# A new prologue for a convolution-and-three-mixes kernel: coefficient tables by full float32 matmuls over nine rows

## The chip, the cores and the metric

The kernel runs on one core of a Trainium2 chip. The metric is the device time of one execution in microseconds (us). Before the change it is 364.62 us, the median of three executions (364.05 to 366.46).

## What is computed

`x` is 128 samples of 64 channels by 1024 positions, all in float32. Four residual layers follow each other. The first is a grouped convolution with nine taps plus a bias that depends on the sample; each of the other three multiplies a sample by a 64 x 64 matrix of its own, which is a softmax-weighted mean of eight given matrices, and adds a bias of its own.

```python
# layer 0
x = x + (conv1d(x, weight, groups=4, pad=4) + (c @ c_weight.T)[:, :, None] + bias[None, :, None])
# layers 1, 2, 3, each with weights of its own
h = gelu(c @ W0 + b0); h = gelu(h @ W1 + b1)
att = softmax(h @ W2 + b2)                      # 128 samples x 8
agg_w = einsum('bk,koi->boi', att, weight)      # 128 matrices of 64 x 64
x = x + (einsum('boi,bih->boh', agg_w, x) + (att @ bias_k)[:, :, None])
```

## The kernel before

The three mixing layers are linear, so each sample needs only the product of its three matrices (each with the identity added) and one bias column. The work has two parts.

**The prologue** makes, for all 128 samples at once, what depends on the condition `c` alone. TensorE runs the three small networks (lines 405 to 421), VectorE and ScalarE the softmax. Then come the *tables* (line 98): `table[n]` holds the 64 x 64 matrix of layer n for every sample. They are made in 24 *banks* (`NTAB`, 8 for each layer), numbered t. A bank is four matmuls (L455) of a piece of `mixtab`, stationary, with the transposed attention `att_t`, moving, into one bank of PSUM (the 2 MiB memory that TensorE writes). Four copies of 64 x 256 then carry it into `table[n]`, on ScalarE (ACT, L576) and VectorE (DVE, L758). `ACT_ALONE` and `DVE_ALONE` name the banks that one of the two copies alone; of every other bank each copies a half. Five banks of PSUM go round, so bank t waits for the copies of bank t-5.

The matmuls of the tables are in the one-pass type fp32r. For accuracy, matrices and attention are each split into a high and a low part, and three products are added by laying the parts in three groups of 9 rows (8 matrices and the identity): partitions 0 to 26 of `mixtab`, with the other partitions set to zero. The rows get there in two steps: `mats` (432 KB) is loaded from memory over 108 partitions, DVE splits it (L710, L712), and three transfers within the chip's SBUF lay it out again, over 9 partitions each (L238). Later the same memory, `mixtab`, holds the `y` tiles of the main loop; so y moves wait for the first eight banks (L243).

**The main loop** goes over 32 steps q of four samples. A step loads `x` (L208), splits it (x_high L514 on ACT, x_low L649 on DVE or L324 on POOL), convolves it in four groups g of six matmuls (`conv`, L360) with the tap matrices `toep_hi` and `toep_lo`, copies the result (L521), moves it within SBUF (L222), composes the sample's matrices (L368, L378), and multiplies (`mix`, L400 to L402). The tap matrices are made in the prologue too: DVE adds an identity (L717), ACT makes the high part (L560) and DVE the low part (L725).

Each engine works its own list in order, and the lists are woven by hand. While the tables are made, `CONV_AFTER` puts a convolution group (q, g) behind a bank, `BIAS_PRODUCTS` and `BIAS_TURNS` put pieces of the bias chain (L430, L434, and `bias_sum`, L693 to L706, on DVE) there, and `SPLIT_AT` the splits of x. `POOL_LOW` names the steps whose low part POOL makes. Once all 24 banks are copied, POOL makes the last inputs of `compose_upper` (L311) and the main loop's first `mix` starts. All transfers go through the one queue of SyncE (SP), in program order.

Of the kernel before, what the change touches and what calls it, by code (L numbers as in the profile page):

```python
# [37 lines left out]
JX = J + 1  # L38
S = 4
# [3 lines left out]
K = 8  # L43
KR = K + 1
PARTS = 3
NL = 3
N = S * J
NH = C // 2
NG = 4
TG = NH // NG  # L50
NTAB = NL * TG
BIAS_TURNS = (4, 12)
BIAS_PRODUCTS = (8, 15)

CONV_AFTER = {1: (0, 0), 2: (0, 1), 3: (0, 2), 4: (0, 3), 9: (1, 0), 11: (1, 1), 13: (1, 2), 14: (1, 3), 19: (2, 0), 22: (2, 1)}
SPLIT_AT = {0: 1, 9: 2, 18: 3}
POOL_LOW = (1,)
ACT_ALONE = (8, 10, 12, 20)
DVE_ALONE = (2, 3, 5, 9, 11)
YHIGH_AT = 19  # L60
CH = 12
CW = NL * NH * 2 * C // CH

# [7 lines left out]
def columns(tile, widths):  # L71

    out, at = {}, 0
    for name, n in widths.items():
        out[name] = tile[:, at:at + n]
        at += n
    return out


def cond_resid_kernel(nc, x_h, net_h, kept_h, row_h, toep_h, mixrow_h, mats_h, out_h):  # L80
    with ExitStack() as ctx:
        def sb(name, shape, dt=F32):
# [31 lines left out]
        mixtab = sb("mixtab", [128, NL, NH, 2 * C], F32R)  # L114
# [6 lines left out]
        att_pad = sb("att_pad", [B, NL, 128], F32R)  # L121
        att_parts = att_pad[:, :, 0:PARTS * KR].rearrange("b n (t k) -> b n t k", t=PARTS)
        att_t = sb("att_t", [128, NL, B], F32R)
# [16 lines left out]
        mats = x_sb[:, 1].rearrange("p g s j -> p (g s j)")[0:KR * CH, 0:CW]  # L140
        mats_hi = conv_sb[:, 1].rearrange("p g n -> p (g n)")[0:KR * CH, 0:CW].bitcast(F32R)
        mats_lo = out_sb[:, 0].rearrange("p s n -> p (s n)")[0:KR * CH, 0:CW].bitcast(F32R)
        vadd = out_sb[:, 0].rearrange("p s n -> p (s n)")[:, CW:CW + C]

        second = columns(out_sb[:, 1].rearrange("p s n -> p (s n)"), dict(TOEP, hid1=NL * B, hid2=NL * B))
        toep, eye_tap = second["toep"], second["eye_tap"]
        toep_all = out_sb[:, 1].rearrange("p s n -> p (s n)")[:, 0:sum(TOEP.values())]
# [9 lines left out]
        net0_in, net_in, kept_in, toep_in, mats_in, mixrow_in, tab_in = (  # L157
            sem(n) for n in ("net0_in", "net_in", "kept_in", "toep_in", "mats_in", "mixrow_in", "tab_in"))
        mats_hi_set, mats_lo_set, parts_zero, parts_set = (
            sem(n) for n in ("mats_hi_set", "mats_lo_set", "parts_zero", "parts_set"))  # L160
        mixtab_zero = sem("mixtab_zero")
# [44 lines left out]
        def _(sp):  # L206
# [36 lines left out]
            sp.wait_ge(tab_ps, TG)  # L243
# [34 lines left out]
        def _(pool):  # L278
            nc.gpsimd.memset(ones[:], 1.0).then_inc(ones_set, 1)
            nc.gpsimd.memset(vcol[:], 1.0).then_inc(ones_set, 1)  # L280
            nc.gpsimd.memset(mixtab[:, 1:].bitcast(F32), 0.0).then_inc(mixtab_zero, 1)
            nc.gpsimd.memset(att_pad[:].bitcast(F32), 0.0).then_inc(parts_zero, 1)
            pool.wait_ge(parts_zero, 1)

            nc.gpsimd.memset(att_parts[:, :, 0::2, K:KR].bitcast(F32), 1.0).then_inc(parts_zero, 1)
            nc.gpsimd.memset(a2_diag[:], 0.0).then_inc(zeros_set, 1)
            nc.gpsimd.memset(a3_diag[:], 0.0).then_inc(zeros_set, 1)
            pool.wait_ge(zeros_set, 2)

# [58 lines left out]
        def _(pe):  # L348
# [87 lines left out]
            pe.wait_ge(parts_set, 2)  # L436
# [10 lines left out]
            pe.wait_ge(tab_in, 16 * PARTS)  # L447
            pe.wait_ge(c0_set, 2)
            for t in range(NTAB):
                n, c = divmod(t, TG)  # L450
                if t >= TB:
                    pe.wait_ge(tab_act, act_banks(t - TB + 1))
                    pe.wait_ge(tab_dve, dve_banks(t - TB + 1))
                for i in range(NG):
                    last = mm(t_bank[t % TB][:, B * i:B * i + B], mixtab[:, n, NG * c + i, :], att_t[:, n, :],  # L455
                              start=True, stop=True)
                last.then_inc(tab_ps, 1)
                if t in CONV_AFTER:
                    q, g = CONV_AFTER[t]
                    conv(q, q % 2, g, banks=2)  # L460
                if t in BIAS_PRODUCTS:
                    bias_products(BIAS_PRODUCTS.index(t) + 1)
                if t in BIAS_TURNS:
                    bias_turn(BIAS_TURNS.index(t))
# [45 lines left out]
        def _(act):  # L510
# [12 lines left out]
            def y_high(q, it, par):  # L523
                act.wait_ge(moved[par], 16 * G * it + 16 * G)
                act.wait_ge(tab_ps, 2 * TG)
                nc.scalar.activation(y_hi[:, par].rearrange("p h s j -> p (h s j)"),
                                     y_sb[:, par].rearrange("p h s j -> p (h s j)"), ACT.Copy).then_inc(yhi_set, 1)
# [27 lines left out]
            for n in range(NL):  # L555
                act.wait_ge(hid2_ps, n + 1)
                nc.scalar.activation(hid2[:, n, :], hid2_bank[n][:, 0:B], ACT.Gelu,
                                     bias=b01[:, 1, n:n + 1]).then_inc(hid2_set, 1)
            act.wait_ge(toep_set, 1)
            nc.scalar.activation(toep_hi[:].rearrange("p d g m -> p (d g m)"), toep,  # L560
                                 ACT.Copy).then_inc(toep_hi_set, 1)
            act.wait_ge(centred, 1)
            nc.scalar.activation(expo[:], expo[:], ACT.Exp).then_inc(exp_set, 1)
            x_high(0, 0, 0)
            act.wait_ge(att_t_ps, 1)
            nc.scalar.activation(att_t[:], bank[7][:, 0:NL * B].rearrange("k (n b) -> k n b", n=NL),
                                 ACT.Copy).then_inc(att_t_set, 1)
# [77 lines left out]
        def _(dve):  # L645
# [42 lines left out]
            def bias_sum(n):  # L688
# [15 lines left out]
                else:  # L704
# [3 lines left out]
            nc.vector.memset(mixtab[:, 0].bitcast(F32), 0.0).then_inc(mixtab_zero, 1)  # L708
            dve.wait_ge(mats_in, 16)
            nc.vector.tensor_copy(mats_hi, mats).then_inc(mats_hi_set, 1)  # L710
            dve.wait_ge(mats_hi_set, 1)
            nc.vector.tensor_tensor(mats_lo, mats, mats_hi.bitcast(F32), ALU.subtract).then_inc(mats_lo_set, 1)  # L712

            dve.wait_ge(toep_in, 16)
            taps = toep.rearrange("p (d g m) -> p d g m", d=2, g=G)
            eyes = eye_tap.rearrange("p (d o m) -> p d o m", d=2, o=1)
            nc.vector.tensor_tensor(taps, taps, eyes.to_broadcast([128, 2, G, 128]), ALU.add).then_inc(toep_set, 1)  # L717
# [6 lines left out]
            dve.wait_ge(toep_hi_set, 1)  # L724
            nc.vector.tensor_tensor(toep_lo[:].rearrange("p d g m -> p (d g m)"), toep,  # L725
                                    toep_hi[:].rearrange("p d g m -> p (d g m)").bitcast(F32),
                                    ALU.subtract).then_inc(toep_lo_set, 1)
# [10 lines left out]
            twice = att[:].unsqueeze(2).to_broadcast([B, NL, 2, K])  # L738
            high = att_parts[:, :, 0::2, 0:K]
            nc.vector.tensor_copy(high, twice).then_inc(parts_set, 1)  # L740
            dve.wait_ge(parts_set, 1)
            nc.vector.tensor_tensor(att_parts[:, :, 1, 0:K], att[:], high[:, :, 0, :].bitcast(F32),
                                    ALU.subtract).then_inc(parts_set, 1)
# [147 lines left out]
```

## Time and profile before

| | us |
|---|---|
| median of three executions | 364.62 |
| the profiled execution, as timed | 365.35 |
| its span in the profile, first to last instruction | 363.5 |

| engine | busy us | share of span |
|---|---|---|
| TensorE matmuls (PE) | 325.5 | 90% |
| its weight loads (PEld, overlap with PE) | 265.4 | 73% |
| VectorE (DVE) | 281.7 | 77% |
| ScalarE (ACT) | 244.4 | 67% |
| GpSimd (POOL) | 138.5 | 38% |

The profile is of one execution. Times are from the span's start. A busy matmul is not a matmul at peak, since matmuls overlap; how far apart two of them start says more. The granted TensorE clock reads 1.00 in every stretch of this profile; how long a piece of equal shape takes tells the two levels apart better here.

### The profile page before, as it was taken

Reading aid. Unit: us, or ns where it says so; the run is one execution under the profiler, and the core shown is the slowest. Engines: PE = TensorE matmul, PEld = TensorE weight load, DVE = VectorE, ACT = ScalarE, POOL = GpSimd, SP = SyncE. Lnnn points to the kernel's source line nnn. Section 1 sums busy time; section 2 is a strip of 40 time slices with the busy share of each in tenths; the row PEclk is TensorE's granted clock in tenths of the full one; section 3 lists DMA queues with packets and bytes.
Section 4 is the critical chain, followed back from the end, with each engine's and each line's share of the span. In section 5 each row is a group of like instructions: output and inputs, shape, how many; then the busy total and the mean of one; then the engine's idle time right before and its main releaser. Section 6 shows DMA issues by size and latency. Waiting matters only on the chain.

```text
span 363.5 us, 6039 instructions
## 1 busy us (share of the span) xinstructions
PE 325.5 (90%) x1542; PEld 265.4 (73%) x1542; DVE 281.7 (77%) x298; ACT 244.4 (67%) x415; POOL 138.5 (38%) x172
## 2 busy tenths in 40 slices
PE   6221999689999999999999999999999999999974
PEld 5101877568888888888888888888888888888862
DVE  5720699968888888888888888888888888888664
ACT  3500699977777777777777777777777777777563
POOL 9000501173444444444444444444444444444100
PEclk9999999999999999999999999999999999999999
DMA  7898165075899899998989898989898989896665
GB/s 255 152 128 141 48 234 199 35 261 206 339 341 339 340 336 339 343 364 324 357 323 356 318 357 314 363 314 361 310 363 304 364 313 368 306 360 263 261 260 231
DMA packets 28927, 104.43 MB, mean 287 GB/s; under 512 B 3206, under 2 KB 3462, under 8 KB 20855
## 3 DMA queue, kind: packets, MB, share of 16 engines
q1 hardware_dynamic: 28919, 104.34, 80.1%
q8 instruction: 3, 0.05, 0.1%
q14 instruction: 5, 0.04, 0.0%
HBM read 35.89 MB, written 33.55 MB: 191 GB/s over the span
## 4 chain that ended last, share of the span: by engine, by line
PE 79%; DMA 8%; DVE 8%; issue 1%; SPq 1%; POOL 1%; ACT 1%; DVEq 0%; POOLq 0%
PE bank L360 46%; PE bank L400 8%; PE bank L401 8%; PE bank L402 8%; DMA mixtab<-out_sb 7%; PE bank L378 4%; DVE table L758 3%; PE bank L368 3%; DMA x_sb<-in_mats 2%; PE bank L455 1%; DVE x_lo L649 1%; POOL a_diag L311 1%; DVE out_sb L684 1%; DVE out_sb L697 1%; DVE mixtab L663 1%
## 5 line engine op out<-in xcount | busy, mean ns | idle before, releaser
L521 ACT ACTIVATE conv_sb<-bank 128x512 f32<-128x512 f32 x128 | 76.5, 599 | 78.7 <-PE bank L360 76.0
L297 POOL COPY a_pair<-table 128x128 f32 (+1 forms) x32 | 61.5, 1921 | 142.2 <-PE bank L368 125.5
L649 DVE TENSOR_TENSOR x_lo<-x_sb,x_hi 128x2064 fp32r<-128x2064 f32 x31 | 71.6, 2308 | 40.5 <-ACT x_hi L514 40.4
L360 PE MATMUL bank<-x_hi,toep_hi 128*128 128x512 f32 x256 | 84.6, 412 | 1.3 <-ACT conv_sb L521 1.3
L360 PE MATMUL bank<-x_lo,toep_hi 128*128 128x512 f32 x256 | 81.1, 398 | 0.0
L360 PE MATMUL bank<-x_hi,toep_lo 128*128 128x512 f32 x256 | 81.0, 398 | 0.0
L663 DVE TENSOR_TENSOR mixtab<-mixtab 128x2048 fp32r<-128x2048 f32 x31 | 70.6, 2279 | 0.0
L546 ACT ACTIVATE out_sb<-bank,beta 128x512 f32<-128x512 f32 x95 | 65.6, 692 | 3.5 <-PE bank L402 3.2
L514 ACT ACTIVATE x_hi<-x_sb 128x2064 fp32r<-128x2064 f32 x32 | 61.4, 1919 | 0.1
L360 PEld LDWEIGHTS bank<-x_hi,toep_lo 128*128 128x128 f32 x256 | 48.6, 190 | 12.0
L360 PEld LDWEIGHTS bank<-x_lo,toep_hi 128*128 128x128 f32 x256 | 48.6, 190 | 11.6
L400 PE MATMUL bank<-mixtab,mix_hi 128*128 128x512 f32 x128 | 53.6, 419 | 3.4 <-DVE out_sb L684 2.3
L360 PEld LDWEIGHTS bank<-x_hi,toep_hi 128*128 128x128 f32 x256 | 45.3, 190 | 9.0 <-ACT conv_sb L521 1.5
L401 PE MATMUL bank<-mixtab,mix_lo 128*128 128x512 f32 x128 | 50.5, 395 | 0.0
L402 PE MATMUL bank<-mixtab,mix_hi 128*128 128x512 f32 x128 | 50.5, 394 | 0.0
L301 POOL COPY a_diag<-table 64x128 f32 (+1 forms) x64 | 42.7, 667 | 9.2 <-POOL a_diag L301 4.6
L658 DVE CAST mixtab<-mixtab 128x2048 fp32r<-128x2048 f32 x29 | 38.0, 1311 | 2.5 <-DMA mixtab<-conv_sb 2.5
L758 DVE COPY table<-bank 64x256 f32<-64x256 f32 x50 | 21.2, 425 | 18.3 <-PE bank L455 17.2
L576 ACT ACTIVATE table<-bank 64x256 f32<-64x256 f32 x46 | 17.2, 375 | 21.5 <-PE bank L455 21.0
L400 PEld LDWEIGHTS bank<-mixtab,mix_hi 128*128 128x128 f32 x128 | 24.3, 190 | 9.9 <-DVE out_sb L684 3.4
L670 DVE TENSOR_SCALAR mix_f<-bank,kept 128x256 f32<-128x256 f32 x64 | 27.6, 470 | 4.0 <-PE bank L378 4.0
L455 PE MATMUL bank<-att_t,mixtab 128*128 128x128 f32 x96 | 14.4, 291 | 16.5 <-DMA mixtab<-out_sb 15.0
(77 smaller groups left out, 306.1 us busy)
## 6 DMA issues: line engine op xcount, KB each, us to landing
x_sb<-in_x SPq DMA_DIRECT2D x32, 1032.0 KB, 5.2
mixtab<-conv_sb SPq DMA_DIRECT2D x128, 256.0 KB, 3.5
out<-out_sb SPq DMA_DIRECT2D x31, 1024.0 KB, 5.5
out<-out_sb SPq DMA_DIRECT2D x2, 512.0 KB, 3.0
mixtab<-conv_sb SPq DMA_DIRECT2D x2, 432.0 KB
out_sb<-in_toep SPq DMA_DIRECT2D x1, 640.0 KB, 6.9
x_sb<-in_mats SPq DMA_DIRECT2D x1, 432.0 KB
mixtab<-out_sb SPq DMA_DIRECT2D x1, 432.0 KB
```

The lines of the kernel that those rows point to most:

```text
L297: nc.gpsimd.tensor_copy(a1_pair[:, par], table[0][:, here, :]).then_inc(pair_in, 1)
L301: nc.gpsimd.tensor_copy(a2_diag[rows, par, :, C * h:C * h + C], table[1][rows, here, :]).then_inc(pair_in, 1)
L360: last = mm(o, w[:, d, g, :], v[:, par, g, :, d:d + J], start=i + d == 0, stop=i + d == 3)
L400: mm(o, m_hi, v_hi, start=True, stop=False)
L401: mm(o, m_lo, v_hi, start=False, stop=False)
L402: mm(o, m_hi, v_lo, start=False, stop=True).then_inc(mix_done, 1)
L514: nc.scalar.activation(x_hi[:, par].rearrange("p g s j -> p (g s j)"), x_sb[:, par].rearrange("p g s j -> p (g s j)"), ACT.Copy).then_inc( ...
L521: nc.scalar.activation(conv_sb[:, par, g, :], conv_ps[g % banks][:, :], ACT.Copy).then_inc(conv_out, 1)
L546: nc.scalar.activation(out_sb[:, par, s, :], mix_ps[s % 2][:, :], ACT.Identity, bias=beta[:, bass.ds(S * q + s, 1)]).then_inc(out_act, 1)
L649: nc.vector.tensor_tensor(x_lo[:, par].rearrange("p g s j -> p (g s j)"), x_sb[:, par].rearrange("p g s j -> p (g s j)"), x_hi[:, par].rea ...
L658: nc.vector.tensor_copy(hi, v).then_inc(yhi_set, 1)
L663: nc.vector.tensor_tensor(lo, v, hi.bitcast(F32), ALU.subtract).then_inc(ylo_set, 1)
```

## The change

The tables are now made by full float32 matmuls, one product in place of three. The matrices go straight from memory to three groups of 9 rows, one for each layer, which start at partitions 0, 32 and 64 of `mrow` (the memory of `out_sb`). The splitting of `mats`, the three transfers within SBUF, the zeroing of `mixtab` and the split of the attention go. The softmax stands ahead of the tap matrices on ACT and DVE, the identity is added to the taps by POOL, `y` has memory of its own (`ybuf`), the taps are loaded into `x_sb[1]` (so that the second x load waits for `toep_lo`), and the woven lists are new.

```diff
-BIAS_TURNS = (4, 12)
-BIAS_PRODUCTS = (8, 15)
-CONV_AFTER = {1: (0, 0), 2: (0, 1), 3: (0, 2), 4: (0, 3), 9: (1, 0), 11: (1, 1), 13: (1, 2), 14: (1, 3), 19: (2, 0), 22: (2, 1)}
-SPLIT_AT = {0: 1, 9: 2, 18: 3}
-POOL_LOW = (1,)
-ACT_ALONE = (8, 10, 12, 20)
-DVE_ALONE = (2, 3, 5, 9, 11)
-YHIGH_AT = 19
-CH = 12
+BIAS_TURNS = (6, 13)
+BIAS_PRODUCTS = (2, 9, 15)
+CONV_AFTER = {5: (0, 0), 6: (0, 1), 7: (0, 2), 8: (0, 3), 11: (1, 0), 12: (1, 1), 14: (1, 2), 15: (1, 3), 19: (2, 0), 21: (2, 1)}
+SPLIT_AT = {2: 1, 11: 2, 18: 3}
+POOL_LOW = (1, 2)
+ACT_ALONE = (0, 1)
+DVE_ALONE = (2, 3)
+YHIGH_AT = 17
+RG = 32
+CH = 4
...
-        att_pad = sb("att_pad", [B, NL, 128], F32R)
-        att_t = sb("att_t", [128, NL, B], F32R)
+        att_pad = sb("att_pad", [B, 128])
+        att_rows = att_pad[:, 0:NL * RG].rearrange("b (n z) -> b n z", n=NL)[:, :, 0:KR]
+        att_t = sb("att_t", [128, B])
...
-            sp.dma_start(mats, mats_h).then_inc(mats_in, 16)
+            for n in range(NL):
+                sp.dma_start(mrow[RG * n:RG * n + KR].rearrange("k (c n) -> k c n", c=CH),
+                             mats_h[KR * n:KR * n + KR, :].rearrange("k (c n) -> k c n", c=CH)).then_inc(tab_in, 16)
+            sp.dma_start(kept[:], kept_h).then_inc(kept_in, 16)
             sp.dma_start(toep_all, toep_h).then_inc(toep_in, 16)
-            sp.dma_start(kept[:], kept_h).then_inc(kept_in, 16)
             load(0, 0)
             sp.dma_start(mixrow, mixrow_h).then_inc(mixrow_in, 16)
-            sp.wait_ge(mixtab_zero, 2)
-            for i, (src, ready) in enumerate(((mats_hi, mats_hi_set), (mats_hi, mats_hi_set), (mats_lo, mats_lo_set))):
-                sp.wait_ge(ready, 1)
-                dst = mixtab[KR * i:KR * i + KR].rearrange("k n c m -> k (n c m)").rearrange("k (c n) -> k c n", c=CH)
-                sp.dma_start(dst.bitcast(F32), src.bitcast(F32)).then_inc(tab_in, 16)
+            sp.wait_ge(toep_lo_set, 1)
             load(1, 1)
...
-            sp.wait_ge(tab_ps, TG)
...
-            nc.gpsimd.memset(mixtab[:, 1:].bitcast(F32), 0.0).then_inc(mixtab_zero, 1)
+            pool.wait_ge(toep_in, 16)
+            nc.gpsimd.tensor_tensor(taps, taps, eyes.to_broadcast([128, 2, G, 128]), ALU.add).then_inc(toep_set, 1)
...
-            for n in range(NL):
-                last = nc.tensor.transpose(bank[7][:, B * n:B * n + B], att_pad[:, n, :].bitcast(F32), ident)
-            last.then_inc(att_t_ps, 1)
-            bias_products(0)
-            pe.wait_ge(toep_hi_set, 1)
-            pe.wait_ge(toep_lo_set, 1)
+            nc.tensor.transpose(bank[7][:, 0:B], att_pad[:], ident).then_inc(att_t_ps, 1)
...
-                    last = mm(t_bank[t % TB][:, B * i:B * i + B], mixtab[:, n, NG * c + i, :], att_t[:, n, :],
+                    rows, at = slice(RG * n, RG * n + KR), 2 * C * (NG * c + i)
+                    last = mm(t_bank[t % TB][:, B * i:B * i + B], mrow[rows, at:at + 2 * C], att_t[rows],
                               start=True, stop=True)
...
+                    if (q, g) == (0, 0):
+                        pe.wait_ge(toep_hi_set, 1)
+                        pe.wait_ge(toep_lo_set, 1)
...
(ACT: exp stands ahead of toep_hi and x_high(0); the copy to att_t leaves ACT)
(DVE: no split of mats, no identity; the order is softmax, att_rows, vrow, vcol, the copy to att_t,
 toep_lo, x_low(0), then the banks; bias_sum(0) is now behind bank 3)
```

## Rows read from the trace of the kernel before

**Rows 1.** Chain that ended last, to 75 us (start us, us, what)

```profile
2.03 5.91 DMA x_sb<-in_mats
...
10.79 24.11 DMA mixtab<-out_sb
...
37.09 2.67 PE bank L360 x6
...
40.18 1.48 PE bank L360 x6
41.66 0.39 PE bank L455 x4
...
47.23 0.91 PE bank L430 x2
...
71.22 2.27 POOL a_diag L311
```

**Rows 2.** Busy time of each engine by stage

```profile
core 0: us, PE busy (x) PEld busy (x) DVE busy (x) ACT busy (x) POOL busy (x), PEclk, DMA share, GB/s
...
10.00:35.00 25.00, 3.49 (x7) 1.12 (x7) 8.43 (x17) 4.87 (x5) 0.00 (x0) 1.00 0.93 125
35.00:71.00 36.00, 31.34 (x169) 26.13 (x169) 30.03 (x60) 30.24 (x62) 6.38 (x7) 1.00 0.38 140
71.00:363.50 292.50, 284.21 (x1342) 232.51 (x1342) 237.76 (x219) 206.08 (x342) 122.95 (x154) 1.00 0.84 320
```

**Rows 3.** Busy time by stage, finer: the transfers before and during the spreading

```profile
6.00:12.00 6.00, 4.52 (x18) 3.60 (x17) 3.52 (x5) 1.82 (x4) 3.73 (x5) 1.00 0.94 309
...
28.00:30.00 2.00, 0.00 (x0) 0.00 (x0) 0.00 (x0) 0.00 (x0) 0.00 (x0) 1.00 1.16 119
```

**Rows 4.** DMA issues: KB each, median us from issue to landing

```profile
x_sb<-in_x SPq DMA_DIRECT2D x1, 1032.0 KB, 10.1
out_sb<-in_toep SPq DMA_DIRECT2D x1, 640.0 KB, 6.9
...
mixtab<-out_sb SPq DMA_DIRECT2D x1, 432.0 KB
...
x_sb<-in_x SPq DMA_DIRECT2D x32, 1032.0 KB, 5.2
```

**Rows 5.** Groups of instructions by line, 35 to 71 us

```profile
L758 DVE COPY table<-bank 64x256 f32<-64x256 f32 x50 | 21.2, 425 | 18.3 <-PE bank L455 17.2
L576 ACT ACTIVATE table<-bank 64x256 f32<-64x256 f32 x46 | 17.2, 375 | 21.5 <-PE bank L455 21.0
...
L521 ACT ACTIVATE conv_sb<-bank 128x512 f32<-128x512 f32 x10 | 6.0, 597 | 2.5 <-PE bank L455 2.4
L514 ACT ACTIVATE x_hi<-x_sb 128x2064 fp32r<-128x2064 f32 x3 | 5.8, 1928 | 0.1
L324 POOL TENSOR_TENSOR x_lo<-x_sb,x_hi 128x2064 fp32r<-128x2064 f32 x1 | 4.6, 4647 | 29.4 <-ACT x_hi L514 29.4
L649 DVE TENSOR_TENSOR x_lo<-x_sb,x_hi 128x2064 fp32r<-128x2064 f32 x2 | 4.6, 2309 | 0.1
```

**Rows 6.** Instructions in order of time, weight loads, prologue and entry (start us, us)

```profile
7.31 1.35 PEld L417 LDWEIGHTS bank<-table,out_sb 128*128 128x128 f32 x6
8.55 0.55 PEld L419 LDWEIGHTS bank<-table 128*128 128x128 f32 x2
9.21 0.50 PEld L420 LDWEIGHTS bank<-row,ones 1*128 1x128 f32 x2
9.82 0.29 PEld L421 LDWEIGHTS bank<-table 128*64 128x64 f32 x2
...
71.07 0.52 PEld L368 LDWEIGHTS bank<-a_pair,a_diag 128*128 128x128 f32 x4 [1.48 <-ACT table L576]
...
71.51 0.30 PEld L360 LDWEIGHTS bank<-x_hi,toep_hi 128*128 128x128 f32 x2
```

**Rows 7.** Instructions in order of time, other engines, prologue

```profile
11.28 1.06 ACT L560 ACTIVATE toep_hi<-out_sb 128x1024 fp32r<-128x1024 f32 x1 [4.04 <-DVE out_sb L717]
...
14.32 0.18 DVE L733 TENSOR_TENSOR att<-expo,recip 128x24 f32<-128x24 f32 x1
```

More of the change, by code:

```diff
@@ L44 @@
 KR = K + 1
-PARTS = 3
 NL = 3
@@ L113, in cond_resid_kernel @@
         toep_lo = sb("toep_lo", [128, 2, G, 128], F32R)
-        mixtab = sb("mixtab", [128, NL, NH, 2 * C], F32R)
+        ybuf = sb("ybuf", [128, 2, 3, S * QP * J], F32R)
         ones = sb("ones", [1, B])
@@ L120, in cond_resid_kernel @@
         att = sb("att", [B, NL, K])
-        att_pad = sb("att_pad", [B, NL, 128], F32R)
-        att_parts = att_pad[:, :, 0:PARTS * KR].rearrange("b n (t k) -> b n t k", t=PARTS)
-        att_t = sb("att_t", [128, NL, B], F32R)
+        att_pad = sb("att_pad", [B, 128])
+        att_rows = att_pad[:, 0:NL * RG].rearrange("b (n z) -> b n z", n=NL)[:, :, 0:KR]
+        att_t = sb("att_t", [128, B])
         vrow = sb("vrow", [B, C])
@@ L134, in cond_resid_kernel @@
         out_sb = sb("out_sb", [128, 2, S, QP * J])
-        y_sb, y_hi, y_lo = (mixtab[:, n].rearrange("p (r h s) j -> p r h s j", r=2, h=QP) for n in range(NL))
+        mrow = out_sb[:].rearrange("p r s n -> p (r s n)")
+        y_sb, y_hi, y_lo = (ybuf[:, :, t].rearrange("p r (h s j) -> p r h s j", h=QP, s=S) for t in range(3))
         y_sb = y_sb.bitcast(F32)
[L140 to L145, printed above, removed]
+        vadd = sb("vadd", [B, C])[:]
+        second = columns(x_sb[:, 1].rearrange("p g s j -> p (g s j)"), dict(TOEP, hid1=NL * B, hid2=NL * B))
         toep, eye_tap = second["toep"], second["eye_tap"]
-        toep_all = out_sb[:, 1].rearrange("p s n -> p (s n)")[:, 0:sum(TOEP.values())]
+        toep_all = x_sb[:, 1].rearrange("p g s j -> p (g s j)")[:, 0:sum(TOEP.values())]
         hid1, hid2 = (second[n].rearrange("p (n b) -> p n b", n=NL) for n in ("hid1", "hid2"))
@@ L155, in cond_resid_kernel @@
         mix_lo = sb("mix_lo", [128, 2, S, 128], F32R)
[L157 to L161, printed above, removed]
+        net0_in, net_in, kept_in, toep_in, mixrow_in, tab_in = (
+            sem(n) for n in ("net0_in", "net_in", "kept_in", "toep_in", "mixrow_in", "tab_in"))
+        parts_zero, parts_set = sem("parts_zero"), sem("parts_set")
         x_in = [sem("x_in0"), sem("x_in1")]
@@ L280, in _ @@
             nc.gpsimd.memset(vcol[:], 1.0).then_inc(ones_set, 1)
-            nc.gpsimd.memset(mixtab[:, 1:].bitcast(F32), 0.0).then_inc(mixtab_zero, 1)
-            nc.gpsimd.memset(att_pad[:].bitcast(F32), 0.0).then_inc(parts_zero, 1)
+            nc.gpsimd.memset(att_pad[:], 0.0).then_inc(parts_zero, 1)
             pool.wait_ge(parts_zero, 1)
-            nc.gpsimd.memset(att_parts[:, :, 0::2, K:KR].bitcast(F32), 1.0).then_inc(parts_zero, 1)
+            nc.gpsimd.memset(att_rows[:, :, K:KR], 1.0).then_inc(parts_zero, 1)
             nc.gpsimd.memset(a2_diag[:], 0.0).then_inc(zeros_set, 1)
@@ L288, in _ @@
             pool.wait_ge(zeros_set, 2)
+            pool.wait_ge(toep_in, 16)
+            taps = toep.rearrange("p (d g m) -> p d g m", d=2, g=G)
+            eyes = eye_tap.rearrange("p (d o m) -> p d o m", d=2, o=1)
+            nc.gpsimd.tensor_tensor(taps, taps, eyes.to_broadcast([128, 2, G, 128]), ALU.add).then_inc(toep_set, 1)
             def lower_mats(q, par):
@@ L434, in bias_turn @@
                 nc.tensor.transpose(bank[5][0:C, 0:B], vrow[:], ident).then_inc(vcol_ps, 1)
-            pe.wait_ge(parts_set, 2)
+            pe.wait_ge(parts_set, 1)
             pe.wait_ge(kept_in, 16)
-            for n in range(NL):
-                last = nc.tensor.transpose(bank[7][:, B * n:B * n + B], att_pad[:, n, :].bitcast(F32), ident)
-            last.then_inc(att_t_ps, 1)
-            bias_products(0)
-            pe.wait_ge(toep_hi_set, 1)
-            pe.wait_ge(toep_lo_set, 1)
+            nc.tensor.transpose(bank[7][:, 0:B], att_pad[:], ident).then_inc(att_t_ps, 1)
             pe.wait_ge(att_t_set, 1)
-            pe.wait_ge(tab_in, 16 * PARTS)
+            pe.wait_ge(tab_in, 16 * NL)
             pe.wait_ge(c0_set, 2)
@@ L459, in _ @@
                     q, g = CONV_AFTER[t]
+                    if (q, g) == (0, 0):
+                        pe.wait_ge(toep_hi_set, 1)
+                        pe.wait_ge(toep_lo_set, 1)
                     conv(q, q % 2, g, banks=2)
                 if t in BIAS_PRODUCTS:
-                    bias_products(BIAS_PRODUCTS.index(t) + 1)
+                    bias_products(BIAS_PRODUCTS.index(t))
                 if t in BIAS_TURNS:
@@ L524, in y_high @@
                 act.wait_ge(moved[par], 16 * G * it + 16 * G)
-                act.wait_ge(tab_ps, 2 * TG)
+                if par == 1:
+                    act.wait_ge(tab_ps, NTAB)
                 nc.scalar.activation(y_hi[:, par].rearrange("p h s j -> p (h s j)"),
@@ L558, in _ @@
                                      bias=b01[:, 1, n:n + 1]).then_inc(hid2_set, 1)
+            act.wait_ge(centred, 1)
+            nc.scalar.activation(expo[:], expo[:], ACT.Exp).then_inc(exp_set, 1)
             act.wait_ge(toep_set, 1)
@@ L561, in _ @@
                                  ACT.Copy).then_inc(toep_hi_set, 1)
-            act.wait_ge(centred, 1)
-            nc.scalar.activation(expo[:], expo[:], ACT.Exp).then_inc(exp_set, 1)
             x_high(0, 0, 0)
-            act.wait_ge(att_t_ps, 1)
-            nc.scalar.activation(att_t[:], bank[7][:, 0:NL * B].rearrange("k (n b) -> k n b", n=NL),
-                                 ACT.Copy).then_inc(att_t_set, 1)
             def table_bank(t):
@@ L706, in bias_sum @@
                     nc.vector.tensor_copy(vdup[:], src.to_broadcast([B, G, 2, CG])).then_inc(vrow_set, 1)
[L708 to L717, printed above, removed]
             logits = bank[4][:, 0:NL * K].rearrange("b (n k) -> b n k", n=NL)
@@ L723, in _ @@
                                     ALU.subtract).then_inc(centred, 1)
[L724 to L727, printed above, removed]
             dve.wait_ge(exp_set, 1)
@@ L737, in _ @@
             dve.wait_ge(att_set, 1)
[L738 to L743, printed above, removed]
+            nc.vector.tensor_copy(att_rows[:, :, 0:K], att[:]).then_inc(parts_set, 1)
             dve.wait_ge(c0_ps, 2)
@@ L747, in _ @@
             nc.vector.tensor_scalar(vcol[0:C, :], bank[6][0:C, 0:B], fcol, None, ALU.add).then_inc(c0_set, 1)
+            dve.wait_ge(att_t_ps, 1)
+            nc.vector.tensor_copy(att_t[:], bank[7][:, 0:B]).then_inc(att_t_set, 1)
+            dve.wait_ge(toep_hi_set, 1)
+            nc.vector.tensor_tensor(toep_lo[:].rearrange("p d g m -> p (d g m)"), toep,
+                                    toep_hi[:].rearrange("p d g m -> p (d g m)").bitcast(F32),
+                                    ALU.subtract).then_inc(toep_lo_set, 1)
             x_low(0, 0)
-            bias_sum(0)
             def table_bank(t):
@@ L768, in _ @@
                 if t - 1 in BIAS_PRODUCTS:
-                    bias_sum(BIAS_PRODUCTS.index(t - 1) + 1)
+                    bias_sum(BIAS_PRODUCTS.index(t - 1))
             y_low(0, 0)
@@ L877 @@
                                   biask[None]]),
-        "mats": np.stack([table_rows(w, n == 0) for n, w in enumerate(ws)], 1).reshape(KR * CH, CW),
+        "mats": np.stack([table_rows(w, n == 0) for n, w in enumerate(ws)]).reshape(NL * KR, NH * 2 * C),
     }
```

1 line of the change is left out of this document (removed).

## Prediction

> **What bounds the kernel now.** I read the chain of work that ended last first [rows 1]. After the load of `mats` it is one transfer, the last of the three within SBUF, from 10.8 to 34.9 us. The stages [rows 2] say what that means: from 10 to 35 us TensorE has 3.5 us of work in 25. From 35 to 71 us the tables are made, with TensorE, DVE and ACT at 31.3, 30.0 and 30.2 us of 36, so no engine has much room. From 71 us on TensorE is busy for 284.2 us of 292.5. That last stage is its own bound and the change leaves its instructions alone; whatever moves the moment when the tables are full (71.0 us; POOL's next work starts at 71.2 [rows 1]) moves the end by the same. So the question is one number: when are the tables full after the change? The span is that number plus 292.5 us. The median of the runs lies 1.1 us above the span (364.62 against 363.5), which I add at the end.
>
> **Start of the tables.** Before, 3 x 432 KB went into 9 partitions at a time. They were issued from 8.9 us on and landed at 34.9, behind some 3 us of x and bias matrix: 1,296 KB in 23 to 26 us, 50 to 56 KB a microsecond. All transfers together moved 119 GB/s then, against 309 GB/s between 6 and 12 us [rows 3]. Now 432 KB go into 9 partitions at a time, and they stand ahead of everything but the networks' weights. By the same rate that is 7.7 to 8.7 us; the other bound is the ordinary rate, 1.4 us. I take 7.7, because the destination has the same shape: from 3.5 to 11.2 us. `kept`, 65 KB, which the transpose of the attention needs, is behind them: 11.7 us.
>
> A page states why the three groups would not help: the Trainium skill ("SBUF — State Buffer", the section on the DMA port swizzle) says that partitions 32 apart share a port and that four neighbours share one, at 27.2 GB/s. By that, an estimate, 8 rows of 16 KB through one port take 4.8 us and the third group goes elsewhere, which would put the sum 2 to 3 us lower; no run here shows the ports.
>
> The softmax no longer waits for DVE's splits and the taps. The logits are done at about 8.8 us (the last loads of L417 and L419 [rows 6]) and eight small instructions of about 0.2 us follow [rows 7]: 10.4. So `kept` decides, a transpose and a copy (0.9 us) follow: the tables start at 12.6 us instead of 35.1, 22.5 us earlier.
>
> **What a bank costs TensorE now.** fp32 goes as two pieces (the two calls of L368 are x4). Four pieces of L368 begin 0.44 us before the next load: 0.11 us each [rows 6]. An fp32r call is one piece, 0.39 us a bank [rows 1]. A bank of four fp32 calls is eight pieces, 0.88 us, at the higher clock (2.4 GHz). At the lower (1.2 GHz) six pieces of L417 take 1.24 us, 0.21 each: 1.7 us a bank. 24 banks cost about 11 us more than before. Fewer rows take nothing off: L420, with one row, is as long as L419.
>
> There is a cost in going between one row and all rows. From L419 to L420 is 0.66 us and on to L421 0.61, where two loads at 0.21 make 0.42 [rows 6]: 0.2 us a change at the lower clock. I take 0.1 at the higher; bounds 0 and 0.2. Some 20 changes between 9 rows and all rows lie behind bank 7: 2 us. The Trainium skill ("TensorEngine Tiling (Array Packing)", Key Properties) says that changing the tiling mode drains TensorE; the trace agrees in kind, and the page has no price.
>
> **The taps and x are now late.** They come behind the slow rows. `toep` (640 KB) took 6.9 us and x 10.1 us from issue to landing [rows 4]. Behind 11.2 us, at 309 GB/s, `kept` and `toep` take 2.3 us and land at 14.0, x(0) another 3.3 less what engines free of rows did meanwhile: 17. POOL adds the identity: half of L324's columns, 2.3 us; the zeroing that kept it busy is gone. 16.4. Then ACT's list: `toep_hi` 1.06 [rows 7] to 17.5, x_high(0) 1.93 [rows 5] to 19.4, and only then bank 0, which ACT must copy alone, four at 0.375: 21.0; bank 1: 22.5. DVE: `toep_lo` to 18.8, x_low(0) 2.31 to 21.8, banks 2 and 3 alone, 1.7 each: 25.2; bias_sum(0) 2.1: 27.4. TensorE makes five banks by about 21 and then waits for bank 0. So of the 22.5 us a good 8 are lost here, and the lower clock of the first banks is hidden behind it.
>
> The second x load now waits for `toep_lo`: issued at 18.8, 5.2 us [rows 4], 24.0. x_high(1) stands on ACT's list ahead of bank 4 and of the copies of the first convolution groups: ACT waits 1.5 us, is done at 25.9, and copies group (0,0) at 28.8 after banks 4 to 6. `CONV_AFTER` gives the groups two PSUM banks, so (0,2) starts at 28.8.
>
> **From there** three lists are nearly equal. TensorE: 16 banks x 0.88 = 14.1, 8 groups x 1.48 = 11.8, two bias products 1.8, turns 0.4, changes 2: 30 us, to 58.8. ACT from bank 6 on: 17 banks x 0.75, 10 copies x 0.6, x_high twice 3.9, y_high 1.9, small ones 0.5: 25.1, to 54. DVE from 27.4: 20 banks x 0.85, two bias sums 4.4, x_low(3) 2.3: 23.7, to 51. Followed bank by bank, TensorE waits little, but y_high(0) and x_high(3) stand on ACT ahead of banks 18 and 19 and x_low(3) on DVE ahead of 20, so that the last banks are copied about 1.8 us after TensorE made them. Tables full: 60.6 us. POOL's two low parts (the second from 40 to 45 us) lie well before their convolutions (bank 11 at about 37, bank 19 at 52), the moves of y and further loads have 10 us and more; those I cost at nothing. If one fell late, TensorE's wait would add up one for one.
>
> The sum: 71.0 - 60.6 = 10.4 us less; span 353.1, time 354.2.
>
> **Rivals.**
> - *The rows are not slow from memory.* For: what slowed down may be the reading of SBUF, which is gone. Against: all transfers beside them were slow together. Rows at the ordinary rate bring taps and x back to 9.3 and 13 us; ACT starts bank 0 at 15, 4.4 us earlier. 350. Chance 0.22.
> - *Everything follows the start:* 22.5 us less, 342. It needs taps, x and copies out of the way; rows 2's three full engines speak against. 0.03.
> - *The woven lists catch.* The second x load takes 10.1 us as the first did, instead of 5.2, and holds ACT ahead of bank 4: 5 us, tables full at 65.5: 359. 0.15.
> - *The gain is eaten and more:* TensorE stays at the lower clock while the tables are made, because nine rows and waits are little work for it. Then a bank is 1.7 us and a group 2.67 [rows 1]: 19 banks, 10 groups and two bias products from 22 us on are 32 + 27 + 2 = 61 us, tables full at about 85: 378. It decides from about 10 us of added time on, when some 40% of this stage ran slow. For: in the prologue before, pieces of the networks stayed at 0.21 us for 7 us. Against: with groups between, the stage rose after 4 us (2.67 to 1.48 us a group [rows 1]). The page "TensorE: Matmul & The Clock Gate" of the Trainium skill (Part 4) says that transposes don't count as busy as matmuls do; nothing here tells how nine rows count. 0.05.
> - *No effect* (the start is earlier but `mix` waits for something else, such as the moves): 0.02.
>
> **How the numbers follow.** My forecast has 0.53 and its own range is 350.5 to 358: changes at 0 or 0.2 us (2 us either way), rows at 8.7 us (+1), the convoy of the last banks. With the rival at 350 and the one at 359 it holds nine tenths, and I take 346 to 360. About 1% is what a measurement of this kernel can tell from no change: faster, below 361.0, gets 0.91 (forecast, first three rivals nearly whole); within 0.04; slower 0.05.
>
> **What would show it.** First table matmul near 12.6 us: right about rows and `kept`; near 11: rows fast. A bank's eight pieces 0.11 us apart, and gaps of 0.1 us at changes. ACT's first table copy near 19.4 us, with `toep_hi` waiting for POOL. POOL's first L311 near 61 us, and a main loop of 292.5 us from there: if that is longer, the shift is given back, and the step that is wrong is the one that says the loop is its own bound.

## The result and the profile after

The changed kernel takes 375.51 us (median of four executions, 374.39 to 386.98) against 365.45 us before (median of the four executions now on record). By the ratio of the comparable executions it is slower by 2.7%: 1.0268, 95% interval 1.021 to 1.0325. The forecast was 354.2 us, faster. The profiled execution took 374.39 us with a span of 372.6 us. One execution of the four, at 386.98 us, fell into a slower state of the chip and is left out of the ratio.

The chain of the kernel after that ended last, its first part (start us, us, what; several instructions merged):

```profile
4.42 13.69 DMA table<-in_mixrow
18.15 2.08 PE bank L428 x2
20.22 5.42 PE bank L449 x24
25.64 2.86 PE bank L358 x6
28.50 2.00 PE bank L449 x8
...
36.29 1.08 PE bank L449 x8
37.38 1.60 PE bank L358 x6
38.98 1.08 PE bank L449 x8
...
41.12 1.98 PE bank L449 x16
...
47.30 2.86 PE bank L358 x6
...
62.37 2.86 PE bank L358 x6
65.22 3.71 PE bank L449 x16
...
84.66 0.47 PE bank L398
```

L449 is a table matmul here and L358 a convolution's. The long idle wait of [rows 1] is gone: after 18.2 us the chain is TensorE almost alone. But the same work has two prices. A bank (x8) is 1.08 us, then 2.00; a convolution group (x6) is 1.60, then 2.86. The stages of the same kernel say when:

```profile
core 0: us, PE busy (x) PEld busy (x) DVE busy (x) ACT busy (x) POOL busy (x), PEclk, DMA share, GB/s
...
35.00:60.00 25.00, 25.00 (x123) 18.61 (x122) 10.43 (x25) 13.25 (x30) 6.31 (x7) 0.86 0.29 106
60.00:80.00 20.00, 20.00 (x74) 16.48 (x73) 12.65 (x20) 11.78 (x23) 3.13 (x4) 0.52 0.19 68
...
100.00:372.60 272.60, 265.94 (x1247) 217.96 (x1245) 220.73 (x203) 188.94 (x313) 110.95 (x135) 0.99 0.86 326
```

From 35 to 80 us TensorE is busy without a break, and DVE and ACT, which had 30 us of work in 36 before [rows 2], are idle for half of the time. The granted clock is 0.86 and then 0.52 of 2.4 GHz: mostly 1.2 GHz in the second stage, although TensorE is never idle there. The low stretches behind 34 us last 6.8 us (from 43.8) and 20.5 us (from 60.9). Before 33 us the column reads 1.00, but there the pieces have the length of the low level: three banks in 5.42 us, a group in 2.86. So TensorE ran at the low level from its first bank up to 33 us as well, and from 18.15 us on it did so without a break. Before, this stage was short of a start; now it is short of TensorE.

The tables are full at 76.6 us (POOL's first L309) instead of 71.2 [rows 1], and the first `mix` begins at 84.66 us (last line of the chain above) instead of 77.15. From there the changed kernel needs 287.9 us and the one before 286.4; a low stretch of the clock among the last matmuls (about 365 to 368 us, where the kernel before has none) stands against the 1.5 us between them. So most of the loss lies where the forecast placed the gain.

The transfers and the first copies went as forecast:

```profile
12.55 5.49 PE L449 MATMUL bank<-att_t,out_sb 9*128 9x128 f32 x24 [0.38 <-DVE att_t L725]
13.04 2.34 POOL L286 TENSOR_TENSOR x_sb<-x_sb 128x1024 f32<-128x1024 f32 x1 [10.74 <-DMA x_sb<-in_toep]
15.41 1.06 ACT L560 ACTIVATE toep_hi<-x_sb 128x1024 fp32r<-128x1024 f32 x1 [5.90 <-POOL x_sb L286]
...
18.80 3.10 ACT L571 ACTIVATE table<-bank 64x256 f32<-64x256 f32 x8
...
26.49 2.78 DVE L695 TENSOR_TENSOR vrow<-vrow,vadd 128x64 f32<-128x64 f32 x1
```

These are from the timeline (start us, us, engine, line, what, idle before and releaser). First table matmul at 12.55 us, forecast 12.6; ACT's first copy at 18.8, forecast 19.4. `kept`, queued behind the slow rows, landed at 11.6 us, forecast 11.7, so the rival with rows at the ordinary rate falls; the second x load took 4.8 us and not 10.1, so the rival at 359 falls too. The last line, an add that takes 2.78 us instead of 0.23, will matter below.

### The profile page after: what moved, and what is told of

Its sections match the earlier page's. It is cut to its first block, busy times and chain, and to the rows that moved or that the text cites. A ratio compares the mean times of both kernels' runs of the same rounds, so it can differ in the third digit from the quotient of the medians.

```text
span 372.6 us, 6214 instructions
## 1 busy us (share of the span) xinstructions
PE 360.1 (97%) x1636; PEld 292.4 (78%) x1636; DVE 275.5 (74%) x291; ACT 245.7 (66%) x416; POOL 138.8 (37%) x173
## 4 chain that ended last, share of the span: by engine, by line
PE 92%; DMA 4%; DVE 1%; SPq 1%; issue 0%; ACT 0%
PE bank L358 51%; PE bank L398 9%; PE bank L449 8%; PE bank L400 8%; PE bank L399 8%; PE bank L376 4%; DMA table<-in_mixrow 4%; PE bank L366 3%; PE bank L428 1%; DVE mix_f L665 0%; DVE out_sb L679 0%; ACT mix_hi L537 0%; DVE ybuf L785 0%; SPq L227 0%; DVE mix_lo L670 0%
## 5 line engine op out<-in xcount | busy, mean ns | idle before, releaser
L295 POOL COPY a_pair<-table 128x128 f32 (+1 forms) x32 | 47.2, 1474 | 127.7 <-PE bank L366 121.3
L358 PE MATMUL bank<-x_hi,toep_hi 128*128 128x512 f32 x256 | 88.1, 426 | 0.0
L358 PE MATMUL bank<-x_lo,toep_hi 128*128 128x512 f32 x256 | 83.9, 410 | 0.0
L358 PE MATMUL bank<-x_hi,toep_lo 128*128 128x512 f32 x256 | 83.7, 409 | 0.0
L658 DVE TENSOR_TENSOR ybuf<-ybuf 128x2048 fp32r<-128x2048 f32 x31 | 71.2, 2296 | 0.0
L358 PEld LDWEIGHTS bank<-x_hi,toep_lo 128*128 128x128 f32 x256 | 50.3, 196 | 12.6
L358 PEld LDWEIGHTS bank<-x_lo,toep_hi 128*128 128x128 f32 x256 | 50.6, 198 | 12.2
L398 PE MATMUL bank<-ybuf,mix_hi 128*128 128x512 f32 x128 | 54.3, 424 | 3.3 <-DVE out_sb L679 2.3
L299 POOL COPY a_diag<-table 64x128 f32 (+1 forms) x64 | 51.3, 802 | 9.2 <-POOL a_diag L299 4.6
L358 PEld LDWEIGHTS bank<-x_hi,toep_hi 128*128 128x128 f32 x256 | 46.5, 196 | 9.3 <-issue 0.9
L400 PE MATMUL bank<-ybuf,mix_hi 128*128 128x512 f32 x128 | 51.1, 399 | 0.0
L399 PE MATMUL bank<-ybuf,mix_lo 128*128 128x512 f32 x128 | 51.0, 399 | 0.0
L653 DVE CAST ybuf<-ybuf 128x2048 fp32r<-128x2048 f32 x29 | 37.4, 1288 | 5.6 <-DMA ybuf<-conv_sb 5.5
L449 PEld LDWEIGHTS bank<-att_t,out_sb 9*128 9x128 f32 x192 | 33.0, 262 | 8.8 <-issue 7.2
L309 POOL COPY a_diag<-table 64x128 f32 (+1 forms) x64 | 27.1, 424 | 32.8 <-DVE table L739 18.0
L449 PE MATMUL bank<-att_t,out_sb 9*128 9x128 f32 x192 | 36.4, 359 | 0.4 <-DVE att_t L725 0.4
```

Of the source, the lines that this page charges most:

```text
L295: nc.gpsimd.tensor_copy(a1_pair[:, par], table[0][:, here, :]).then_inc(pair_in, 1)
L299: nc.gpsimd.tensor_copy(a2_diag[rows, par, :, C * h:C * h + C], table[1][rows, here, :]).then_inc(pair_in, 1)
L358: last = mm(o, w[:, d, g, :], v[:, par, g, :, d:d + J], start=i + d == 0, stop=i + d == 3)
L398: mm(o, m_hi, v_hi, start=True, stop=False)
L399: mm(o, m_lo, v_hi, start=False, stop=False)
L400: mm(o, m_hi, v_lo, start=False, stop=True).then_inc(mix_done, 1)
```

## The experiments

Two theories stood against each other. A: the matmuls over nine rows are why the clock isn't granted in full. B: it is the float32 type with its two pieces a call, or the waits between banks.

**Nine rows become 128.** `mrow` is zeroed before the rows land, and the attention of layer n is in a slab of its own that is zero outside rows 32n to 32n+8. The instructions of a bank, their number and their type stay. The zeroing and two more transposes come with it, and the tables start 1.2 us later. The main lines:

```diff
-                    rows, at = slice(RG * n, RG * n + KR), 2 * C * (NG * c + i)
-                    last = mm(..., mrow[rows, at:at + 2 * C], att_t[rows],
+                    at = 2 * C * (NG * c + i)
+                    last = mm(..., mrow[:, at:at + 2 * C], att_t[:, n, :],
```

> Tables by the same full float32 matmuls (eight pieces a bank), but over all 128 rows: the rows outside the layer's nine are zero. Theory A (nine rows are too little work for TensorE's clock): the clock stays at the high level once it has risen, a bank takes 0.88 us throughout, the tables are full near 62 us and the time is 354 to 358. Theory B (it is the float32 type, two pieces a call, or the waits between banks, not the rows): the clock falls as after the change, tables full near 76 us, time 374 to 377.

Measured: 358.56 us (357.94 to 359.14), ratio to the kernel before 0.9801 (0.9745 to 0.9858). Rows of zeros turn a loss of 2.7% into a gain of 2.0%, 0.6 us short of the range that A had been given. In its chain:

```profile
33.71 0.89 PE bank L453 x8
34.60 1.41 PE bank L360 x6
36.01 0.89 PE bank L453 x8
...
49.73 0.91 PE bank L453 x8
...
63.20 1.05 PE bank L368 x4
```

The bank is at 0.89 us from 33.7 on; it stays there but for the pieces near 63 us, behind a wait of 2 us. Theory B falls: type, pieces and waits are all still there. And a bank is 0.89 us instead of 1.08 at the same level of the clock: something besides the clock is gone too, see the 64 rows below.

The start differs as well. Right behind the first three banks, here and in the changed kernel:

```profile
18.94 1.02 PE L430 MATMUL bank<-table,vcol 65*128 65x512 f32 x2
19.80 2.84 PE L453 MATMUL bank<-att_t,out_sb 128*128 128x128 f32 x24
```

```profile
18.15 2.08 PE L428 MATMUL bank<-table,vcol 65*128 65x512 f32 x2
20.15 5.49 PE L449 MATMUL bank<-att_t,out_sb 9*128 9x128 f32 x24
```

Over 128 rows the high level is there from 18.9 us on, over nine rows from 33. The 128-row kernel then loses a part of it again: it waits 3.48 us for the bias turn at 29.85 us, and the clock is low until 32.5.

**The kernel before, over 27 rows.** The opposite edit on the other kernel: its fp32r matmuls over the 27 rows that hold something.

```diff
-mixtab[:, n, NG * c + i, :], att_t[:, n, :],
+mixtab[0:PARTS * KR, n, NG * c + i, :], att_t[0:PARTS * KR, n, :],
```

> The kernel before, with its fp32r table matmuls over the 27 rows that hold something instead of 128. Theory A: fewer rows let the clock fall in the table stage (35 to 71 us), at least where four banks follow each other; if all of it ran at the low level it would add some 27 us, if a third some 9: 366 to 380. Theory B: nothing changes, 364.6, since the type and the order are those of before.

Measured: six executions, 371.1, 375.7 and four from 379.4 to 379.9. Even the fastest, which is the profiled one, is more than 3 us above the slowest of the kernel before that ran beside it (367.7). By stages:

```profile
54.00:64.00 10.00, 10.00 (x52) 7.11 (x51) 7.75 (x15) 8.11 (x21) 0.87 (x3) 1.00 0.39 152
64.00:74.00 10.00, 10.00 (x33) 7.71 (x31) 9.13 (x17) 9.76 (x18) 0.87 (x3) 0.50 0.37 132
```

The clock is at half for ten microseconds with TensorE busy throughout (and for some 3.4 us from 50 on), where the profile of the kernel before reads 1.00. Type and order were those of before: only the rows had changed. With the first experiment this shows from both sides that the number of rows is what mattered. A bank alone between groups is 0.59 us here at the high level where it was 0.39, the same 0.2 us as between 1.08 and 0.89.

**Convolutions spread.**

```diff
-... 8: (0, 3), 11: (1, 0), 12: (1, 1), 14: (1, 2), 15: (1, 3), 19: (2, 0), 21: (2, 1)}
+... 8: (0, 3), 10: (1, 0), 12: (1, 1), 14: (1, 2), 16: (1, 3), 18: (2, 0), 20: (2, 1)}
```

> The changed kernel with the convolution groups of banks 11 to 21 behind every second bank (10, 12, 14, 16, 18, 20) instead of 11, 12, 14, 15, 19, 21, so that at most two banks come without a group. Theory A: shorter stretches of nine-row work, so the clock falls for less of the stage (it was low for 6.8 and 20.5 us after 34 us): 360 to 370. Theory B: as after the change, 374 to 377.

Measured: two executions at 371.2 and 371.3 us and two at 379.2 and 379.6. The lower pair is some 4 us below the changed kernel, the upper pair 4 us above it. In the profiled execution (371.2) the clock was high from 29 to 53 us and low from there to 77, one long stretch for two shorter ones. The expectation of 360 to 370 failed.

**Two fillers behind nine banks.** The filler is a matmul over 128 rows and 512 columns of `toep_hi` into the PSUM bank that the next convolution starts afresh.

```diff
+                    mm(conv_ps[g % 2][:, :], toep_hi[:, 0, 0, :], toep_hi[:, 0].rearrange("p g m -> p (g m)"),
+                       start=True, stop=True)     # FILL = 2 times
```

> The changed kernel with two matmuls over 128 rows and 512 columns that compute nothing of use behind each of nine banks that have no convolution (18 in all, 0.235 us each at the high level, 4.2 us together). Theory A: the clock stays high from 34 us on, and with 4.2 us of filler the tables are full near 66 us: 359 to 363, faster in spite of more work. Theory B: the clock falls all the same and the fillers cost 0.43 us each, 7.7 us: about 382.

Measured: 374.4, 376.7 and 379.3 us, and one execution of 388.3; ratio 1.0294 (1.0211 to 1.0377). Not what A had been made to say. The profile is of the execution of 388.3 us, so it can't stand for the others; in it the clock fell, for longer than without fillers. Either A was wrong or the dose was too small, so the dose was raised.

**Six fillers.** `FILL = 6`.

> The changed kernel (nine rows) with six filler matmuls instead of two behind each of nine banks, 1.4 us each time, as long as a convolution group; 12.7 us of filler at the high level. If work over all rows in equal parts keeps the clock up: tables full near 75 us, time 368 to 372, no longer than with two fillers (378). If it doesn't, the fillers cost 23 us at the low level and the time is above 390.

Measured: 376.18 us (two executions), ratio 1.0289 (1.0224 to 1.0353). The time missed what was expected (368 to 372), but the stages of this kernel show what two fillers did not bring, a full clock through the whole stage, with the tables still over nine rows:

```profile
34.00:60.00 26.00, 26.00 (x133) 19.09 (x133) 9.79 (x22) 12.68 (x27) 5.94 (x6) 1.00 0.26 93
60.00:84.00 24.00, 24.00 (x128) 18.53 (x128) 13.51 (x22) 12.82 (x25) 3.43 (x6) 1.00 0.19 67
```

54 fillers, 12.7 us of them, cost no more time than 18, since all else ran at the high level. Bought this way it costs what it gives. Part of the miss is the change of rows: a filler stretch and the bank behind it are 1.58 and 1.08 us where 1.36 and 0.89 would be without it, some 3 us over the nine stretches.

**73, 64 and 32 rows.** The 128-row kernel, its table matmuls over fewer rows. 73 rows take all three groups in. 64 and 32 are a half and a quarter of the array's rows.

```diff
-mrow[:, at:at + 2 * C], att_t[:, n, :],
+mrow[0:2 * RG + KR, at:at + 2 * C], att_t[0:2 * RG + KR, n, :],                                  # 73
+mrow[64 * (n // 2):64 * (n // 2) + 64, at:at + 2 * C], att_t[64 * (n // 2):64 * (n // 2) + 64, n, :],   # 64
+mrow[RG * n:RG * n + RG, at:at + 2 * C], att_t[RG * n:RG * n + RG, n, :],                         # 32
```

> The 128-row kernel (358.56 us) with its table matmuls over rows 0 to 72, the fewest that hold all three groups and still more than half of the rows. Theory A1 (the clock follows how many rows a matmul spans): it falls for some more of the stage, 360 to 370. Theory A2 (what counts is the change between small and whole row groups, which this kernel doesn't have: a bank stays at 0.89 us): the clock is as with 128 rows, 357 to 360.

> The 128-row kernel with the table matmuls over 64 rows: 0 to 63 for layers 1 and 2, 64 to 127 for layer 3. Rows 0 to 72 kept the time (358.3) and a bank at 0.89 us; 32 rows did not (366 to 374, a bank 1.08). If the number of rows decides, 64 is nearly 73: 357 to 362. If leaving and entering a smaller row group decides, it is like 32 rows: 366 to 374, with a bank at 1.08 us.

> The 128-row kernel with its table matmuls over the layer's whole group of 32 rows, 23 of them zero. A1: 32 rows are nearly as little as nine, or somewhat better: 368 to 376. A2: as with nine rows, 374 to 376, a bank 1.08 us at the high level. If rows of zeros count for nothing and only the mode does, the same; if the number of rows spanned counts in proportion, the low stretches (27 us after the change) shrink only a little.

Measured: 358.26 us (357.1 to 359.46) over 73 rows, 362.51 (361.6 to 363.24) over 64. Over 32 rows it is 365.6, 368.6 and 373.8, and one execution of 645.6 that belongs to no comparison. Zeroing, transposes and start are the same in all of them and in the 128-row kernel, so between these the rows alone differ. The chain over 64 rows and then the one over 73, the same stretch:

```profile
31.14 1.62 PE bank L360 x6
...
33.95 1.62 PE bank L360 x6
35.57 1.08 PE bank L453 x8
```

```profile
32.88 1.43 PE bank L360 x6
...
35.20 1.41 PE bank L360 x6
36.61 0.89 PE bank L453 x8
```

Both kernels had the high clock from 30.5 us on, the 64-row one all the way to 351 us, the 73-row one but for 64.7 to 68 us, with waits. Yet a bank and a group together are 2.69 us with 64 rows and 2.31 with 73. That is the price of the two changes between a smaller and the whole set of rows, 0.19 us each at the high level, and no matter of the clock. It is paid by the stretch and not by the bank: in the changed kernel one bank between groups is 1.08 us and two in a row are 1.98, so the second is 0.90. Over the stage it makes the 4.2 us between 362.5 and 358.3. So the 64-row kernel meets neither expectation in full, and the two effects come apart: with 64 rows the change is paid and the clock stays; with 32, in the profiled execution (368.6), it came up only at 39.6 us and fell twice, near 47 and near 63 us. From 64 rows (362.5) to nine (375.5) are 13 us.

The start is another matter. Over 73 and 64 rows TensorE stayed at the low level until about 30 us, 11 us longer than over 128. That 73 rows cost no more time than 128 is in part luck: the 128-row kernel lost the lead again at its bias turn, for which the 73-row one did not wait.

**The bias turn two banks later.** The 128-row kernel still stood at 358.6, 4.4 us over the forecast, and TensorE idled 3.5 us from 26 us on, waiting for the turn.

```diff
-BIAS_TURNS = (6, 13)
-BIAS_PRODUCTS = (2, 9, 15)
+BIAS_TURNS = (8, 13)
+BIAS_PRODUCTS = (2, 10, 15)
```

> The 128-row kernel with the first bias turn behind bank 8 instead of 6 and the second bias product behind bank 10 instead of 9, so that TensorE does not wait for vrow. There VectorE stood 3.2 us in an add (L699) while POOL made x_lo(1), TensorE idled 3.5 us, and the clock was low from 29.1 to 32.5. If that stall was on the path: 2.5 to 4 us less, 355 to 356, and no low stretch near 30 us. If the copies behind it absorb the gain: 358.

Measured: 355.81 us (354.94 to 356.51), ratio 0.9729 (0.9681 to 0.9778), 2.8 us less. A part of it is the clock, which no longer falls near 30 us. POOL's first upper copy is at 60.68 us: the tables are full where the forecast had them (60.6), and the time is 1.6 us over the forecast. The agreement is partly chance, since this kernel starts its tables 1.4 us later and has none of the row changes, for which the forecast counts 2 us.

```profile
60.68 3.38 POOL L311 COPY a_diag<-table 64x128 f32<-64x128 f32 x4 [12.77 <-DVE table L745]
```

**The same turn with nine rows.** The edit above on the changed kernel alone.

> The changed kernel (nine rows) with the later bias turn and product alone. With 128 rows it was worth 2.8 us, where TensorE stood waiting at the high level. With nine rows TensorE at the low level is behind the vector engine there and hardly waits: 373 to 376, no gain beyond the spread of its runs.

Measured: 383.24 us (379.74 to 384.19), ratio 1.047 (1.0418 to 1.0522): 8 us slower than the changed kernel, which no theory had said (expected was no gain, 373 to 376). The stages show one low stretch of 50 us where there had been 6.8 and 20.5:

```profile
40.00:90.00 50.00, 49.52 (x157) 38.15 (x158) 20.66 (x38) 20.86 (x41) 8.84 (x9) 0.50 0.19 69
```

With the same matmuls in a slightly other order the clock didn't come back for the middle of the stage. TensorE had waited 0.74 us for `vcol` just before 40.5 us, where the stretch begins; in the changed kernel the clock fell at 43.8 us without a wait. Whether that wait matters, and why just this order is worse, stays open.

**y_high(0) late**, behind bank 22 (`YHIGH_AT = 22`), on the 128-row kernel with the later turn.

> The 128-row kernel with the later bias turn (355.81 us), and y_high(0) behind bank 22 instead of 17 on ScalarE, so that x_high(3), x_low(3) and the last copies come earlier. VectorE ended the tables at 60.5 us after waiting 0.8 us for x_high(3): at most 0.8 to 1.9 us less, 354 to 355.5; if ScalarE then ends the tables as late as VectorE did, no change, 355.8.

Measured: 354.89 us (353.91 to 355.15), ratio 0.9708 (0.9677 to 0.974). The step from 355.81 is 0.9 us, near the spread of the runs, but POOL's first upper copy moved by as much, from 60.68 to 59.92 us. This is the best of the versions, 10.5 us below the kernel before by medians and 20.6 below the changed one.

**x_lo(1) on VectorE** (`POOL_LOW = (2,)`), on that kernel.

> The kernel of e10_yhigh_late (354.89 us) with x_lo(1) made by VectorE instead of POOL. In every kernel with POOL at work on x_lo(1) the small add of bias_sum(0) (128x64, two SBUF inputs) stood 2.8 to 3.2 us instead of 0.23, until POOL was done. If POOL's instruction is what held it, the add takes 0.23 us again; VectorE does 2.3 us more, so bias_sum(0) ends about 1 us earlier than now and the time is 353.5 to 355.5. If something else held it, the add stays at 3 us and the time grows by some 2 us, 356 to 357.

Measured: 355.2 us (354.11 to 355.77), ratio 0.9715 (0.9667 to 0.9763), no different. But the add: first the kernel with x_lo(1) on POOL, then this one.

```profile
26.42 3.35 DVE L699 TENSOR_TENSOR vrow<-vrow,vdup 128x64 f32<-128x64 f32 x1
```

```profile
25.51 2.31 DVE L648 TENSOR_TENSOR x_lo<-x_sb,x_hi 128x2064 fp32r<-128x2064 f32 x1 [0.48 <-ACT x_hi L515]
...
29.69 0.23 DVE L699 TENSOR_TENSOR vrow<-vrow,vdup 128x64 f32<-128x64 f32 x1
```

POOL's long instruction had held it: in the first kernel it ran from 25.08 to 29.68 us and the add ended at 29.77. The sum of the two orders is the same: VectorE works 2.3 us on x_lo(1) or stands 3.1 us behind POOL.

## Why the prediction was wrong, point by point

- **What bounded the kernel before; the main loop its own bound: right in the main.** From the first `mix` on the kernels need 286.4 and 287.9 us. By the prediction's own sign, the time from POOL's first upper copy on, it is 296.0 us for 292.5: 3.5 us longer, 2.0 of them ahead of the first `mix`, with the clock low until 81.4 us, and 1.5 at the end. The instructions are the same; that a low clock can reach into this part was not in the sum.
- **The rows, `kept`, the start of the tables: right** (12.55 us for 12.6). The estimate of 4.8 us for the rows, which the prediction gives beside its own 7.7, did not come out: `kept`, behind them, landed at 11.6 us. That taps and x come late behind the slow rows was right as well: ACT copied from 18.8 us (19.4 forecast), so that a third of the 22.5 us is lost at once.
- **The price of a bank at either level: right for a bank by itself** (0.89 us in the 128-row kernel for 0.88; 5.42 us for three banks at the low one for 5.1, 0.3 of it a change of rows).
- **The changes of row group: a term too small.** I took 0.1 us each from a measured 0.2 at the low level, by halving. It is 0.19 at the high level and 0.29 at the low one (a bank 2.00 us for 1.71); about 4 us in the stage instead of 2. The high end of its bounds was the right value.
- **The level of the clock: the step that failed.** The forecast was summed at the high level, with "the lower clock of the first banks is hidden" ahead of it, and the slow case got 0.05. Both halves failed. The low level was not hidden: TensorE worked without a break from 18.15 us on, at the low level until 33. And the clock fell again for 6.8 and 20.5 us. The argument against it was that the clock had risen between groups before. But the banks between those groups were over 128 rows, most of them zero, and this was the very thing that the change took away. "Fewer rows take nothing off" was true of the length of an instruction and was read as if it were true of all. The rival named nine rows as the mechanism, but priced it as all or nothing: 378 us with the whole stage low. It was low up to 33 us and for 27 of the next 47, and that is 375.5.
- **"Followed bank by bank, TensorE waits little": missed one wait, which cost nothing in the changed kernel.** The add behind POOL took 2.8 us and ended at 29.3 us, but TensorE, at the low level, came to the bias turn only at 33.15. Over 128 rows it got there sooner and waited; moving the turn was worth 2.8 us. The rule is in the Trainium skill ("SBUF — State Buffer", Who interferes with whom): a DVE instruction with two SBUF inputs contends with a GpSimd one that reads SBUF. The last experiment agrees, 3.35 against 0.23 us. I costed POOL's low part at nothing because its result was early, and didn't ask whom it stops.
- **The sum, repaired, in the profiled execution.** Forecast span 353.1. Group (0,2) starts at 34.7 us instead of 28.8: +5.9. (The 128-row kernel with the later turn had it at 28.3, with the clock high from about 19 us.) From there to the last bank are 40.8 us instead of 30.0. At the high level it would be about 31.0, an estimate from the six-filler kernel, which took 44.6 us for it, 13.6 of them fillers and their changes: +1.0 for the work, +9.8 for the low stretches. The copies end 1.1 us behind the last bank and not 1.8: -0.7. With that the tables are full at 76.6 us. The 3.5 us of the first point lead to 372.6, the measured span. So the low clock makes 5.9 and 9.8 of the 19.5 us, and it stands beside the 3.5. The median lies 21.3 us over the forecast: 0.7 more because the runs lie 1.8 us above the span instead of 1.1, and 1.1 because the profiled execution was the fastest.

## What to carry to other kernels

Before narrowing a matmul to the rows that hold data, look at what fills the stage. Here matmuls over nine rows, in a stage made mostly of them, went with a TensorE clock at half while the engine was never idle, and rows of zeros that seemed wasted were worth 17 us (375.5 to 358.6), 13 of them from nine rows to 64. Price separately the change between a small and the whole set of rows (0.19 us here, each way). And for each long GpSimd instruction that a plan adds, ask which two-input VectorE instructions fall into its span.

## What the runs showed of the hardware

- A busy TensorE can have the low clock. In the changed kernel it was busy 20.00 of 20.00 us at a granted clock of 0.52. With table matmuls over 9, 27 and 32 rows the clock fell in the table stage; over 64 rows it held from 30.5 us to 351, and over 73 and 128 it fell only in short stretches with waits. In the float32 kernels the rise came between 18.8 and 20 us in the four with 128 rows, and at about 29 us or later with fewer. The added rows held zeros only.
- With six fillers over 128 rows behind nine of the banks, the clock read 1.00 from 34 to 84 us although the banks were over nine rows.
- Where the clock falls is unstable: executions of one kernel with few rows lie apart (371 and 379 us for the spread convolutions), those of the float32 tables over 73 and 128 rows within 2.4 us. Moving one bias turn and one bias product, 0.2 and 1 us of work, made 8 us.
- Going between 64 rows or fewer and all rows costs 0.19 us each way at the high level; between 73 and all it costs nothing that shows (a bank 0.89 us as with 128).
- The profile's clock can read 1.00 where it was low. The changed kernel's banks take 2.00 us up to 33 us in a stretch where the column says 1.00; in the six-filler kernel the same pieces, as long, read 0.50. The length of a known piece tells more.
- A VectorE add with two SBUF inputs stood 3.35 us beside a GpSimd instruction of 4.6 us and took 0.23 us without it.
